# Recurrent layer inputs: step sizes computed once with tokens on partitions and spread by TensorE, B and C split once on all partitions

## The reference

```
xz = x @ in_proj_w.T + in_proj_b ; x_main, z = split(xz)
xc = silu(causal_conv_width_4(x_main) + conv_b)
ssm = xc @ x_proj_w.T + x_proj_b            # 33 columns per token
B_t, C_t = ssm[..., :16], ssm[..., 16:32]
delta = softplus(ssm[..., -1:])             # one step size per token
h = exp(A * delta) * h + delta * B_t * x_t  # per token, 256 channels by 16 states
y = sum_n(h * C_t) + D * x_t ; y = y * silu(z) ; out = y @ out_proj_w.T + ...
```

## Time and profile before

| | |
|---|---|
| median of 3 runs | 2642.61 us (2636.57 to 2643.38) |
| the profiled execution's own time | 2648.85 us |
| its span, first to last instruction | 2647.0 us |
| mean granted TensorE clock | 0.867 |
| first instruction of `scan_inputs` | 1062.15 us |
| end of its last VectorE instruction | 1160.50 us |

### The profile page before, as it was taken

One profiled execution on the slowest core, in us unless ns is written; L12 is line 12 of the kernel. 1 busy time (PEld: TensorE's weight loads), 2 busy tenths in 40 slices (PEclk: granted clock), 3 DMA queues, 4 the chain that ended last, 5 costly groups with the idle time before them and its releaser, 6 DMA issues. The chain is left out here.

```text
span 2647.0 us, 35471 instructions
## 1 busy us (share of the span) xinstructions
PE 2102.6 (79%) x11888; PEld 1380.2 (52%) x11912; DVE 1704.8 (64%) x4085; ACT 1021.6 (39%) x2225; POOL 495.3 (19%) x843
## 2 busy tenths in 40 slices
PE   6696999976997895547774996597599869988788
PEld 3453888853554444112222454486333346766677
DVE  5565677764675556789997455456689665655655
ACT  2353222211564451444441343321177723443333
POOL 0331111001111420226662331010211000000000
PEclk8597999986897797679997798799699879999989
DMA  8320000003111310000001320001311010000000
GB/s 314 98 57 13 1 1 1 1 24 96 49 49 36 96 45 0 0 0 0 0 0 63 95 44 13 0 1 42 119 41 43 23 40 1 0 0 0 0 1 17
DMA packets 60046, 94.41 MB, mean 36 GB/s; under 512 B 11312, under 2 KB 33136, under 8 KB 58736
## 3 DMA queue, kind: packets, MB, share of 16 engines
q1 hardware_dynamic: 29792, 55.57, 6.2%
q0 software_dynamic: 29952, 36.45, 5.7%
q10 hardware_dynamic: 144, 0.39, 0.1%
HBM read 65.63 MB, written 31.29 MB: 37 GB/s over the span
## 5 line engine op out<-in xcount | busy, mean ns | idle before, releaser
L904 DVE TENSOR_REDUCE m<-banks 128x1 f32<-128x512 f32 (+3 forms) x512 | 272.6, 584 | 80.1 <-PE banks L1057 53.5
L2435 PEld LDWEIGHTS banks<-w_ffn,eh 128*128 128x128 f32 x2144 | 280.1, 191 | 21.7
L2435 PE MATMUL banks<-w_ffn,eh 128*128 128x128 f32 x2144 | 281.7, 275 | 0.0
L1325 DVE TENSOR_REDUCE m<-banks 128x2 f32<-128x308 f32 x384 | 164.3, 475 | 173.2 <-PE banks L1604 97.2
L1025 ACT ACTIVATE p<-banks 128x512 f32<-128x512 f32 (+3 forms) x512 | 233.7, 522 | 97.0 <-PE banks L1103 56.6
L2423 PE MATMUL banks<-x_hi,w_hi 128*128 128x512 f32 x472 | 211.7, 448 | 18.7 <-PEq L330 18.7
L1055 PE MATMUL banks<-K,Qf 32*128 32x512 f32 (+2 forms) x512 | 181.1, 511 | 38.1 <-PEq L330 33.2
L2425 PE MATMUL banks<-x_hi,w_lo 128*128 128x512 f32 x472 | 188.7, 400 | 0.0
L2424 PE MATMUL banks<-x_lo,w_hi 128*128 128x512 f32 x472 | 188.0, 398 | 0.0
L2405 ACT ACTIVATE et<-banks 128x512 f32<-128x512 f32 x140 | 83.7, 598 | 248.5 <-PE banks L2425 198.2
L2715 POOL TENSOR_TENSOR hc<-sh,cb 128x1024 f32<-128x1024 f32 x64 | 153.1, 2393 | 113.6 <-ACT cb L2730 108.0
(11 more groups left out here) (398 smaller groups left out, 4293.1 us busy)
## 6 DMA issues: line engine op xcount, KB each, us to landing
Qf<-stack_q_plain POOLq DMA_DIRECT2D x48, 256.0 KB, 3.0
Qf<-stack_q_masked POOLq DMA_DIRECT2D x32, 256.0 KB, 3.0
K<-stack_k_self POOLq DMA_DIRECT2D x32, 256.0 KB, 3.1
w_ffn<-ffn_dram SPq DMA_DIRECT2D x1, 6144.0 KB, 35.7
stack_q_plain<-q_hi SPq DMA_DIRECT2D x24, 256.0 KB, 3.5
stack_q_masked<-q_hi SPq DMA_DIRECT2D x16, 256.0 KB, 2.9
stack_k_self<-k_hi SPq DMA_DIRECT2D x16, 256.0 KB, 3.1
K<-stack_k_ctx POOLq DMA_DIRECT2D x48, 80.0 KB, 2.6
```

The lines of the kernel that those rows point to most:

```text
L904: ins = dve.reduce_max(k.m[:, t, h:h + 1], bank[:, 0:(t + 1) * P if k.kind == "page" else S], AX)
L1325: dve.reduce_max(k.m[:, t:t + 2, h], first_banks[c % 3][:].rearrange("p (a k) -> p a k", a=2)[:, :, 0:S2], AX).then_inc(sem("max_done"), 1)
L2435: last = pe.matmul(bank[:, t * P:(t + 1) * P], k.h[:, n % RING, t * P:(t + 1) * P], w(down.format(e))[:, i * P:(i + 1) * P], start=(i == 0 ...
```

## The change

The step sizes are computed with tokens on partitions. TensorE takes 128 tokens of `xc` as the stationary operand and one column of weights as the moving one, so that the 2048 step sizes fill a 128 x 16 corner of `ps[5]`. VectorE and ScalarE work on that corner once, after the last batch. VectorE then lays each batch's 4 columns out as four diagonal 128 x 128 matrices (`diag`), and TensorE multiplies them by a matrix of ones, which puts the row on all partitions; ScalarE copies it to `k.dt`. B and C of all batches are collected in one bank (`ps[4]`, batch b at partitions 32b), biased and split into three parts once on 128 partitions, and ScalarE copies the 12 pieces of 32 x 512 to their places in `k.bc`. The order of the steps of a batch changes too.

```diff
-    "m_xp_b": (1, lambda i: i["L2_attn_x_proj_b"][0:32].reshape(32, 1)),
+    "m_xp_b": (1, lambda i: np.tile(i["L2_attn_x_proj_b"][0:32].reshape(32, 1), (4, 1))),
...
-    raw, e, ln, d, iz = (sb(name, [P, S]) for name in ("raw", "e", "ln", "d", "iz"))
+    bf, parts = sb("bf", [P, S]), sb("bparts", [P, 3, S], BF16)
+    raw, e, ln, d, iz, dt = (sb(name, [P, B * QT]) for name in ("raw", "e", "ln", "d", "iz", "dtp"))
+    diag = sb("diag", [P, 2, QT, P])
...
             convolve(0)
-            activate(0)
-            convolve(1)
             for b in range(B):
-                split(b)
                 if b + 1 < B:
-                    activate(b + 1)
-                step_sizes(b)
-                if b + 2 < B:
-                    convolve(b + 2)
+                    convolve(b + 1)
+                activate(b)
+
+            dve.wait_ge(sem("dt_done"), B)
+            ch.link(dve.tensor_scalar(raw[:], dt_bank[:, 0:B * QT], w("m_dt_b"), None, ALU.add))
+            dve.scalar_tensor_tensor(e[:], raw[:], -1.0, raw[:], ALU.mult, ALU.max).then_inc(sem("abs_ready"), 1)
+
+            dve.wait_ge(sem("bc_done"), B)
+            ch.link(dve.tensor_scalar(bf[:], bc_bank[:], w("m_xp_b"), None, ALU.add))
+            for part in range(3):
+                dve.tensor_copy(parts[:, part], bf[:]).then_inc(sem("part_ready"), 1)
+                dve.wait_ge(sem("part_ready"), part + 1)
+                if part < 2:
+                    ch.link(dve.tensor_tensor(bf[:], bf[:], parts[:, part], ALU.subtract))
...
+            for b in range(B):
+                if b >= 2:
+
+                    dve.wait_ge(sem("spread_done"), b - 1)
+                dve.tensor_tensor(diag[:, b % 2], over(w("ident"), 1, QT), over(dt[:, b * QT:(b + 1) * QT], 2, P), ALU.mult).then_inc(sem("diag_ready"), 1)
...
             first_tap(0)
-            activate(0)
-            gate(0)
-            first_tap(1)
             for b in range(B):
-                logarithms(b)
-                if b + 1 < B:
-                    activate(b + 1)
-                    gate(b + 1)
+                gate(b)
+                if b == 0:
+                    first_tap(1)
+                activate(b)
                 if b + 2 < B:
                     first_tap(b + 2)
...
+            for part in range(3):
+                act.wait_ge(sem("part_ready"), part + 1)
+                for b in range(B):
+                    last = nc.scalar.copy(k.bc[32 * part:32 * part + 32, b * S:(b + 1) * S], parts[32 * b:32 * b + 32, part])
+                last.then_inc(sem("part_placed"), 1)
+            for b in range(B):
+                act.wait_ge(sem("spread_done"), b + 1)
+                nc.scalar.copy(k.dt[:, b], ps[b][:]).then_inc(sem("dt_ready"), 1)
...
+            def parameters(b):
+                pe.wait_ge(sem("xc_ready"), b + 1)
+                for t in range(QT):
+                    for i in range(2):
+                        last = pe.matmul(dt_bank[:, b * QT + t:b * QT + t + 1], k.xc[:, b, i, t * P:(t + 1) * P], w("m_dt")[:, i * P:i * P + 1],
+                                         start=(b == 0 and t == 0 and i == 0), stop=(i == 1), skip_group_check=True)
+                last.then_inc(sem("dt_done"), 1)
...
-                if b >= 1:
-
-                    pe.wait_ge(sem("dt_ready"), b)
...
+            for b in range(B):
+                pe.wait_ge(sem("diag_ready"), b + 1)
+                for t in range(QT):
+                    last = pe.matmul(ps[b][:, t * P:(t + 1) * P], w("ones"), diag[:, b % 2, t, :], start=(t == 0), stop=True, skip_group_check=True)
+                last.then_inc(sem("spread_done"), 1)
```

More of the change, by code:

```diff
@@ L2480, in scan_inputs @@
     c, z, zt, t = sb("c", [P, 2, 2, S]), sb("z", [P, 2, S]), sb("zt", [P, 2, S]), sb("st", [P, 2, S])
-    bf, bh = sb("bf", [32, S]), sb("bh", [32, S], BF16)
-    raw, e, ln, d, iz = (sb(name, [P, S]) for name in ("raw", "e", "ln", "d", "iz"))
+    bf, parts = sb("bf", [P, S]), sb("bparts", [P, 3, S], BF16)
+    raw, e, ln, d, iz, dt = (sb(name, [P, B * QT]) for name in ("raw", "e", "ln", "d", "iz", "dtp"))
+    diag = sb("diag", [P, 2, QT, P])
     cw, cbias, zbias = sb("cw", [P, 8]), sb("cbias", [P, 2]), sb("zbias", [P, 2])
+    bc_bank, dt_bank = ps[4], ps[5]
     with nc.Block() as block:
@@ L2490, in _ @@
             dve.memset(xp[:, :, :, 0:NCONV - 1], 0.0)
-            dve.memset(k.bc[:], 0.0)
+            dve.memset(k.bc[96:P, :], 0.0)
             dve.tensor_scalar(cw[:], w("m_conv"), 0.5, None, ALU.mult)
@@ L2508, in activate @@
                 dve.scalar_tensor_tensor(k.xc[:, b], t[:], 1.0, c[:, b % 2], ALU.add, ALU.mult).then_inc(sem("xc_ready"), 1)
[L2510 to L2535, removed]
@@ new lines, in _ @@
+            dve.wait_ge(sem("log_ready"), 1)
+            ch.link(dve.tensor_scalar(iz[:], d[:], -1.0, 0.0, ALU.add, ALU.is_equal))
+            ch.link(dve.scalar_tensor_tensor(d[:], d[:], -1.0, iz[:], ALU.add, ALU.add))
+            ch.link(dve.reciprocal(d[:], d[:]))
+            dve.tensor_tensor(ln[:], ln[:], iz[:], ALU.add)
+            ch.link(dve.tensor_tensor(d[:], d[:], e[:], ALU.mult))
+            ch.link(dve.tensor_tensor(d[:], d[:], ln[:], ALU.mult))
+            ch.link(dve.scalar_tensor_tensor(dt[:], raw[:], 0.0, d[:], ALU.max, ALU.add))
@@ L2548, in _ @@
+            for b in range(B):
+                if b >= 2:
+                    dve.wait_ge(sem("spread_done"), b - 1)
+                dve.tensor_tensor(diag[:, b % 2], over(w("ident"), 1, QT), over(dt[:, b * QT:(b + 1) * QT], 2, P), ALU.mult).then_inc(sem("diag_ready"), 1)
+            dve.wait_ge(sem("diag_ready"), B)
         @block.gpsimd
@@ L2585, in activate @@
                 nc.scalar.activation(t[:], c[:, b % 2], ACT.Tanh).then_inc(sem("tanh_c"), 1)
[L2587 to L2593, removed]
             act.wait_ge(sem("halved"), 1)
             first_tap(0)
-            activate(0)
-            gate(0)
-            first_tap(1)
             for b in range(B):
-                logarithms(b)
-                if b + 1 < B:
-                    activate(b + 1)
-                    gate(b + 1)
+                gate(b)
+                if b == 0:
+                    first_tap(1)
+                activate(b)
                 if b + 2 < B:
                     first_tap(b + 2)
+            act.wait_ge(sem("abs_ready"), 1)
+            nc.scalar.activation(e[:], e[:], ACT.Exp, scale=-1.0).then_inc(sem("e_ready"), 1)
+            act.wait_ge(sem("e_ready"), 1)
+            nc.scalar.activation(d[:], e[:], ACT.Identity, bias=1.0).then_inc(sem("e1_ready"), 1)
+            act.wait_ge(sem("e1_ready"), 1)
+            nc.scalar.activation(ln[:], d[:], ACT.Ln).then_inc(sem("log_ready"), 1)
+            for part in range(3):
[6 more added lines that the diff above has]
+                nc.scalar.copy(k.dt[:, b], ps[b][:]).then_inc(sem("dt_ready"), 1)
+            act.wait_ge(sem("dt_ready"), B)
+            act.wait_ge(sem("part_placed"), 3)
         @block.tensor
@@ L2619, in project @@
                     pe.matmul(ps[i][:], w("m_in")[:, i * P:(i + 1) * P], x, start=True, stop=True).then_inc(sem("in_done"), 1)
+            def parameters(b):
[5 more added lines that the diff above has]
+                last.then_inc(sem("dt_done"), 1)
+                for i in range(2):
+                    last = pe.matmul(bc_bank[32 * b:32 * b + 32, :], w("m_xp")[:, i * 32:(i + 1) * 32], k.xc[:, b, i], start=(i == 0), stop=(i == 1))
+                last.then_inc(sem("bc_done"), 1)
             project(0)
@@ L2624, in _ @@
                     project(b + 1)
-                pe.wait_ge(sem("xc_ready"), b + 1)
-                if b >= 1:
-                    pe.wait_ge(sem("dt_ready"), b)
[L2629 to L2634, removed]
+                parameters(b)
+            pe.wait_ge(sem("xm_ready"), 2 * B)
+            pe.wait_ge(sem("z_ready"), 2 * B)
+            for b in range(B):
[3 more added lines that the diff above has]
+                last.then_inc(sem("spread_done"), 1)
     end_of_block(net)
```

## The result

The changed kernel took 2636.83 us (median of 20 runs, 2625.35 to 2643.04), the kernel before 2647.45 us (median of 20 runs, 2636.28 to 2657.32). The ratio is 0.9954, interval 0.9941 to 0.9967: 8.7 to 15.6 us faster.

The account below looks back on a forecast made before the run. VectorE was taken to bound the block before, a serial chain afterwards. First activation 8.1 us later, two rounds of 22.2 and 28.2 to the end gave 5.1 us gain, from the 2642.61 median to 2637 us; range 2623 to 2649.

Parts of the forecast that it names:

- A0: VectorE's activation of the first batch, after two convolutions; claimed to end at 1082.8, 8.1 us later than before.
- the two rounds: From the first batch's activation to the third's, the serial chain run twice; claimed 22.2 us each.
- the end: From the third batch's activation to the block's last instruction; claimed 28.2 us.
- the ring: Serial chain between successive activations through TensorE, ScalarE and VectorE; 17.5 us undisturbed, 22.2 with GpSimd's products.
- Q: TensorE's matmuls after each activation: 16 one-column rows, claimed 3.4 us at low clock, then four rows for B and C.
- The turns with GpSimd: GpSimd's two products and VectorE's convolution taps wait for each other's current instruction; claimed 4.7 us more per round.
- The slower rival: TensorE's one-column matmuls cost 0.36 us per row, not 0.214; 6.5 us slower than before, 2649 us; chance 0.16.
- The rival with fast thin rows: TensorE's one-column rows run at the high clock or load faster; gain 22 us, 2620 us; chance 0.08.
- VectorE keeps its turn: Through all six convolution taps, only one GpSimd product gets in; round 19.9 us, gain 9.7, 2633 us; chance 0.18.
- no meeting costs anything: GpSimd's products do not delay VectorE's convolutions; rounds of 17.5 us, gain 18, 2624 us; chance 0.08.
- The sign: Expected in the profile after: VectorE busy for about 35 us of the block in place of 77.7.
- The spread: TensorE's 16 matmuls putting step sizes on all partitions near the block's close; 32 rows at 0.29 us, claimed 9.3 us.

Follow-up runs that it names:

- the second experiment: Changed kernel, but GpSimd's two products wait for their batch's activation on VectorE, and ScalarE's last activation precedes its last gate; block 77.35 us, ratio 0.9901.

## Why the prediction came out as it did

The predicted 2637 and the range held the time. That the number is so near is partly luck: it was counted from a median of 2642.61 over three runs, and twenty gave 2647.45. The gain is the better test. I predicted 5.1 us, the block gave 14.5, the runs 8.7 to 15.6. My most likely class, no measurable change (0.52), was wrong; faster had 0.38. Mechanism and order of the steps were right, and three terms were too high: A0 by 0.9 us, the two rounds by 3.1, the end by 5.3. These 9.3 us and the predicted 5.1 make the 14.5 of the block, to a tenth.

- *VectorE's load does not set the time, the ring does.* Right. VectorE's work fell by 33.6 us, the block by 14.5. Taking Q out of the ring gave 17 us, lengthening Q took 3.6 us per round.
- *A0 is later by 8.1 us.* It was 7.2: C0 and C1 took 12.67 us together, 4.0 more than their twelve taps alone, and not 4.7.
- *A round is 22.2 us.* It was 20.8 and 20.6. The turns with GpSimd cost 4.1 and not 4.7 us, and the taps start sooner: the eight dense rows of Q and P took 5.4 us (about 3.4 and 2.0) and not 5.9, since the projections ran at the high clock, and from their end to C's start it was 2.2 us and not 2.5. Two rounds: 3.1 us.
- *A matmul of one column costs 0.214 us per row at the low clock.* Right: 3.58 us for 16 rows at a granted clock of 0.50, and 3.55 for the added 16; from start to start it is 0.21 us. The slower rival is gone with it. The rival with fast thin rows is gone for Q0 to Q2 and held for Q3, 1.95 us at 1.00.
- *Two products meet each C and exclude its taps in turns.* Shown by the taps of 2.77 and 2.82 us above and by the second experiment; the two rivals in which VectorE keeps its turn, or no meeting costs anything, fall. The Trainium skill, "SBUF — State Buffer", section "Who interferes with whom", says that a VectorE instruction with two SBUF inputs contends with a GpSimd instruction that reads SBUF. Here the trace agrees: 8.42 us for six taps beside two products, 4.31 without.
- *From A2 to the end 28.2 us.* It was 22.9 (24.2 to the next block's first instruction, of which the barrier is 1.3 to 1.4 both times). Q3 came out 1.3 us shorter, at the high clock. The spread took 5.69 us and not 9.3.
- *VectorE busy for about 35 us of the block.* It was 44.15. The sign counted the taps at their undisturbed length, and the profile counts their waits as busy; without the meetings it was 32.09. The 45 us stated for step sizes and split were low too: their groups in the trace of before add up to about 54 us. No term of the sum uses either.
- *0.29 us per row in the spread.* This is the term that failed most. I took it at the low clock from four rows of L2752. In the spread the first 13 rows took 2.74 us at a granted clock of 0.50, and the last ones ran at 1.00:

```profile
1137.76:1140.50 2.74, 2.74 (x13) 2.74 (x14) 1.11 (x2) 2.68 (x5) 0.00 (x0) 0.50 0.03 6
...
1142.50:1143.40 0.90, 0.90 (x8) 0.76 (x7) 0.00 (x0) 0.54 (x1) 0.00 (x0) 1.00 0.00 0
```

That is 0.21 us per row, the price of a thin row, and 0.11 at the high clock. In the six experiments the 32 rows took 5.5 to 6.5 us. The four rows of L2752 say the same once they are read row by row. The first two of them, the first three, and all four:

```profile
1413.71 0.80 PE L2752 MATMUL banks<-w_attn,gated 128*128 128x128 f32 x2
1413.71 1.01 PE L2752 MATMUL banks<-w_attn,gated 128*128 128x128 f32 x3
1413.71 1.22 PE L2752 MATMUL banks<-w_attn,gated 128*128 128x128 f32 x4
```

Each further row adds 0.21 us. But the next matmul, L2753, starts 1.15 us after the first row and not 0.85: a change between the two kinds of matmul costs some 0.3 us per group of four. I divided that 0.3 by four and then multiplied it by 32, though the spread has no such changes. The rival of 0.36 us per thin row was built on the same rows.

The recurrence behind the block was untouched: 257.8 us before and after.

## What to carry to other kernels

When work leaves the engine that bounds a block, look at once for the cycle of waits that will bound it next, and walk it with the new order of every queue: here the contents were worth 29 us and the order that came with them took half back. Work that is ready early belongs ahead of a wait in an in-order queue: two projections moved ahead of one wait gave 17 us where TensorE was in the cycle, and nothing where it was not. Place GpSimd's products where VectorE idles and not where it streams, which gave 7.9 us here. And when a price per row is read from a short group, look at what one more row adds before it is multiplied.

## What the runs showed of the hardware

- VectorE's taps and GpSimd's products take turns instruction by instruction: with two products inside C2 or C3, the six taps took 8.37 to 8.44 us in the three kernels of that order, and each of these products lasted 2.67 to 2.86 us and not 2.34 to 2.42. With one product in the way it was 6.3 to 6.45.
- A float32 matmul of one column costs as much per row as one of 8 or, in the spread, 128: 0.21 us from start to start at a granted clock of 0.50 (3.58 us for 16 rows of one column, 3.42 for 16 of eight, 2.74 for 13 of 128). At 1.00 it was 0.12 (1.95 us for 16 rows of one column) and 0.11 (of 128).
- At 0.50 a change from a group of such rows to matmuls of another kind and back cost some 0.3 us (L2752, 1.15 us from group start to the next kind, four rows of 0.21).
- Whole-run times of this program scatter by 18 to 21 us over 20 runs. In the eight profiled executions the parts outside the block differ by 9 and 13 us, while the block took 70.65 and 71.09 us where two kernels had the same chain.
